# Row lists of a routed feed-forward layer: one-hot products with the operands exchanged

## The reference, cut to what matters

```python
logits = xf @ Wr + br                      # (4096, 8)
Sm = softmax(logits, axis=-1)
G_t, idx_t = top_k(Sm.T, n_tok // E)       # 512 tokens of each expert
tokens = xf[idx]                           # gather
mid = silu(einsum('keh,ehf->kef', tokens, Wu) + bu)
out = einsum('kef,efh->keh', mid, W_down) + b_down
y = zeros_like(xf).at[idx].add(G[..., None] * out)
```

## Time and profile before

| | us |
|---|---|
| median of 3 runs (lowest, highest) | 440.31 (439.63, 442.09) |
| profiled execution | 442.52 |
| its span, first to last instruction | 440.6 |

### The profile page before, as it was taken

The page is one execution under the profiler, slowest core; times in us unless marked ns, Lnnn a source line. Parts: engine busy times, 40 slices in busy tenths (PEclk is TensorE's granted clock), DMA queues, the critical chain, the costliest instruction groups (busy, mean ns, idle before and its releaser), DMA issues.

```text
span 440.6 us, 5594 instructions
## 1 busy us (share of the span) xinstructions
PE 364.5 (83%) x1631; PEld 241.7 (55%) x1631; DVE 235.1 (53%) x882; ACT 147.7 (34%) x350; POOL 165.2 (37%) x250
## 2 busy tenths in 40 slices
PE   5899999899998980112599999999999999999920
PEld 3788886567775650002337566474655657464610
DVE  2555553787889888887753736513130311059450
ACT  1433332344685884330031120402213030347600
POOL 0310053001467884000343442436334253564853
PEclk9999998999999995555589999989999999999985
DMA  8845443600133554800111352514433162689641
GB/s 276 285 137 177 156 126 117 218 2 1 48 121 105 185 178 137 9 0 2 49 49 51 79 114 61 82 51 99 118 81 50 45 131 87 112 280 372 222 145 48
DMA packets 49631, 50.75 MB, mean 115 GB/s; under 512 B 12138, under 2 KB 42563, under 8 KB 49603
## 3 DMA queue, kind: packets, MB, share of 16 engines
q1 hardware_dynamic: 43650, 40.32, 30.2%
q0 software_dynamic: 5952, 10.10, 11.4%
HBM read 32.97 MB, written 17.43 MB: 114 GB/s over the span
## 4 chain that ended last, share of the span: by engine, by line
PE 62%; DVE 14%; POOL 10%; issue 6%; DMA 3%; ACT 1%; POOLq 0%; SPq 0%; DVEq 0%; ACTq 0%
PE ps L808 16%; PE ps L779 15%; PE ps L614 6%; PE ps L622 6%; PE ps L598 6%; PE ps L753 4%; PE ps L692 3%; POOL rstd L1390 3%; DVE qexp L1016 2%; PE ps L705 2%; DMA out<-h_all 1%; PE ps L766 1%; DMA heads<-ysum,idx 1%; POOL ysum L1443 1%; DVE ht_all L1132 1%
## 5 line engine op out<-in xcount | busy, mean ns | idle before, releaser
L808 PE MATMUL ps<-wdn_s,ht_all 128*128 128x256 f32 (+1 forms) x384 | 97.0, 399 | 0.0
L779 PE MATMUL ps<-xgt,wup_s 128*128 128x512 f32 (+1 forms) x192 | 88.7, 615 | 0.0
L808 PEld LDWEIGHTS ps<-wdn_s,ht_all 128*128 128x128 f32 (+1 forms) x384 | 68.9, 192 | 25.5 <-issue 18.4
L1338 ACT ACTIVATE ht_all<-ps,bup_s 128x512 f32<-128x512 f32 (+1 forms) x48 | 33.0, 687 | 126.8 <-PE ps L779 126.8
L1436 POOL DMA_INDIRECT xg<-table,idx x32 | 32.4, 1013 | 92.1 <-DVE idx L1139 54.1
L779 PEld LDWEIGHTS ps<-xgt,wup_s 128*128 128x128 f32 (+1 forms) x192 | 33.7, 184 | 47.9 <-issue 47.9
L1443 POOL DMA_INDIRECT ysum<-yb,idx x24 | 40.6, 1690 | 48.2 <-DVE yb L1170 42.7
L1170 DVE TENSOR_SCALAR yb<-ps,gate 128x256 f32<-128x256 f32 x24 | 11.6, 484 | 57.4 <-PE ps L808 57.4
L598 PE MATMUL ps<-wqkv_s,heads 128*128 128x264 f32 x128 | 33.1, 406 | 7.0 <-DMA heads<-xt 5.2
L705 PE MATMUL ps<-wp_s,turned 128*128 128x264 f32 x128 | 33.7, 385 | 0.0
L598 PEld LDWEIGHTS ps<-wqkv_s,heads 128*128 128x128 f32 x128 | 25.5, 201 | 11.9 <-issue 7.3
(11 more groups left out here) (189 smaller groups left out, 519.1 us busy)
## 6 DMA issues: line engine op xcount, KB each, us to landing
wdn_s<-wdn SPq DMA_DIRECT2D x8, 640.0 KB
heads<-xt SPq DMA_DIRECT2D x8, 512.0 KB, 3.7
h_all<-x SPq DMA_DIRECT2D x8, 512.0 KB, 5.9
ht_all<-xtq SPq DMA_DIRECT2D x8, 512.0 KB, 3.7
table<-x SPq DMA_DIRECT2D x32, 128.0 KB, 1.7
ysum<-x SPq DMA_DIRECT2D x32, 128.0 KB, 1.8
h_all<-ysum SPq DMA_DIRECT2D x8, 512.0 KB, 8.7
out<-h_all SPq DMA_DIRECT2D x8, 512.0 KB, 6.1
```

What stands on the lines that cost most here:

```text
L779: mm = pe.matmul(ps[0:width, f % 2, :], wup_s[:, c, f * P:f * P + width], xgt[:, c, :], start=(c == 0), stop=(c == C - 1))
L808: mm = pe.matmul(ps[:, bank, 0:D], mid[0:rows_, f, j * P:(j + 1) * P], wdn_s[0:rows_, f, :], start=(f == 0), stop=(f == FT - 1))
L1338: act.activation(mid[0:width, f, :], ps[0:width, f % 2, :], ACT.Silu, bias=bup_s[0:width, e // GS, f:f + 1]).then_inc(s_mid, 1)
```

## The change

A slot is split into 64 partition parts and 8 column parts. `hot` has 64 one-hot values for each tile (128 x 2048), `pay` 16 columns. In the 32 products the operands are exchanged: 16 columns of `pay` are the weights, and 64 columns of `hot`, 64 bytes apart, are streamed, into 16 partitions x 64 columns of PSUM. ScalarE copies this (`keep_shares`) into a memory that is free by then; two f32 products with the 16 x 64 shares as weights and 8 constant columns (C_ROWS) turn it into 64 partitions each, once into the lower and once into the upper half. `numbers` reads 8 columns as before. In an expert the order on TensorE is `shared_lists(e + 2)`, `turn(e + 1)`, `whole_lists(e + 2)`; in expert 2 the second part stands behind the second row block of the down product, and `numbers(4)` behind the second product with the gates.

```diff
+KD = 2 * KT
+SLOTS = KSEL // KD
...
+    for half in range(2):
+        for value in range(2):
+            for j in range(KT):
+                c[value * KD + half * KT + j, C_ROWS + half * KD + value * KT + j] = 1.0
...
-        hot = dead[:, FT * KSEL:FT * KSEL + NT * P // 2].bitcast(BF16).rearrange("p (k s) -> p k s", s=NT)
-        iotas = sb("iotas", [P, P, NT], BF16)
+        hot = dead[:, FT * KSEL:FT * KSEL + NT * SLOTS // 2].bitcast(BF16).rearrange("p (k s) -> p k s", s=NT)
+        iotas = sb("iotas", [P, SLOTS, NT], BF16)
...
-        eq4 = sb("eq4", [P, NT, KT])
-        pay = sb("pay", [P, NT, 2, KT], BF16)
+        eq4 = sb("eq4", [P, NT, KD])
+        pay = sb("pay", [P, NT, 2, KD], BF16)
...
+        shares = junk[0:2 * KD, 4, 0:SLOTS]
...
-            def lists(e):
+            def shared_lists(e):
                 pe.wait_ge(s_hot, e + 1)
                 for s in range(NT):
-                    mm = pe.matmul(ps[:, 6, 0:2 * KT], hot[:, :, s], pay[:, s].rearrange("p w k -> p (w k)"),
+                    mm = pe.matmul(ps[0:2 * KD, 6, 0:SLOTS], pay[:, s].rearrange("p w k -> p (w k)"), hot[:, :, s],
                                    start=(s == 0), stop=(s == NT - 1))
+                mm.then_inc(s_sharemm, 1)
+
+            def whole_lists(e):
+                pe.wait_ge(s_share, e + 1)
+                for half in range(2):
+                    at = C_ROWS + half * KD
+                    mm = pe.matmul(ps[half * SLOTS:(half + 1) * SLOTS, 6, P:P + KD], shares, cs[0:2 * KD, at:at + KD],
+                                   start=True, stop=True)
                 mm.then_inc(s_idmm, 1)
...
                 if e + 2 < E and e != 2:
-                    lists(e + 2)
+                    shared_lists(e + 2)
                 if not last:
                     turn(e + 1)
+                if e + 2 < E and e != 2:
+                    whole_lists(e + 2)
...
                     if e == 2 and j == 0:
-                        lists(4)
-
-            lists(0)
+                        shared_lists(4)
+                    if e == 2 and j == 1:
+                        whole_lists(4)
+
+            shared_lists(0)
+            whole_lists(0)
             for r in range(2):
                 count_second(r)
             turn(0)
-            lists(1)
+            shared_lists(1)
+            whole_lists(1)
...
-                dve.tensor_scalar(part_i[:], slot_i[:], KT.bit_length() - 1, None, ALU.arith_shift_right).then_inc(s_slot, 1)
-                dve.tensor_scalar(four_i[:], slot_i[:], KT - 1, None, ALU.bitwise_and).then_inc(s_slot, 1)
+                dve.tensor_scalar(part_i[:], slot_i[:], KD.bit_length() - 1, None, ALU.arith_shift_right).then_inc(s_slot, 1)
+                dve.tensor_scalar(four_i[:], slot_i[:], KD - 1, None, ALU.bitwise_and).then_inc(s_slot, 1)
...
-                dve.tensor_tensor(hot, part.to_broadcast([P, P, NT]), iotas[:], ALU.is_equal).then_inc(s_hot, 1)
+                dve.tensor_tensor(hot, part.to_broadcast([P, SLOTS, NT]), iotas[:], ALU.is_equal).then_inc(s_hot, 1)
...
-                dve.tensor_copy(idp[:], ps[:, 6, 0:2 * KT]).then_inc(s_idp, 1)
+                dve.tensor_copy(idp[:], ps[:, 6, P:P + KD]).then_inc(s_idp, 1)
...
-                    if e == 2 and j == 0:
+                    if e == 2 and j == 1:
                         numbers(e + 2)
...
+            def keep_shares(e):
+                act.wait_ge(s_sharemm, e + 1)
+                act.copy(shares, ps[0:2 * KD, 6, 0:SLOTS]).then_inc(s_share, 1)
+
             def expert(e):
                 for f in range(FT):
                     up(e, f)
+                if e + 2 < E and e != 2:
+                    keep_shares(e + 2)
                 turn(e + 1)
+                if e == 2:
+                    keep_shares(e + 2)
 
             act.sem_inc(s_mid, 2)
+            keep_shares(0)
             turn(0)
+            keep_shares(1)
...
-            pool.tensor_copy(iotas[:], cs[:, C_IOTA:C_IOTA + P].unsqueeze(2).to_broadcast([P, P, NT])).then_inc(s_iotas, 1)
+            pool.tensor_copy(iotas[:], cs[:, C_IOTA:C_IOTA + SLOTS].unsqueeze(2).to_broadcast([P, SLOTS, NT])).then_inc(s_iotas, 1)
```

More of the change, by code:

```diff
@@ L79 @@
 C_FOUR = C_HEAD8 + HH
-C_TILE = C_FOUR + KT
+C_TILE = C_FOUR + KD
 C_PART = C_TILE + NT
@@ L85 @@
 C_PICK = C_NEG + 2 * TB
-C_ALL = C_PICK + P
+C_ROWS = C_PICK + P
+C_ALL = C_ROWS + 2 * KD
 R_BK, R_BP, R_GAMMA, R_BETA = (D * i for i in range(4))
@@ L109, in constants @@
     c[:, C_HEAD8:C_HEAD8 + HH] = p[:, None] // HD == np.arange(HH)
-    c[:, C_FOUR:C_FOUR + KT] = np.arange(KT)
+    c[:, C_FOUR:C_FOUR + KD] = np.arange(KD)
     c[:, C_TILE:C_TILE + NT] = np.arange(NT)
@@ L359, in build @@
         s_idmm = sem("s_idmm")
+        s_sharemm = sem("s_sharemm")
+        s_share = sem("s_share")
         s_idp = sem("s_idp")
@@ L1121, in spread @@
             def spread(e):
-                shape = [P, NT, KT]
+                shape = [P, NT, KD]
                 part = part_f[:, e:e + 1, :]
                 dve.tensor_tensor(eq4[:], four_f[:, e, :].unsqueeze(2).to_broadcast(shape),
-                                  cs[:, C_FOUR:C_FOUR + KT].unsqueeze(1).to_broadcast(shape), ALU.is_equal).then_inc(s_eq4, 1)
+                                  cs[:, C_FOUR:C_FOUR + KD].unsqueeze(1).to_broadcast(shape), ALU.is_equal).then_inc(s_eq4, 1)
                 dve.wait_ge(s_eq4, e + 1)
```

## The result

The kernel with the change took 462.63 us (median of 4 runs, 461.44 to 464.62), the kernel before beside it 440.87 (4 runs, 439.63 to 442.09): a ratio of 1.0494, with a 95% interval of 1.0453 to 1.0536. That is 21.8 us slower, where 12.1 were forecast. The profiled execution took 462.39 us, its span is 460.6. Where the clock fell is known from this execution alone; its mean granted clock is 0.899, that of the other three runs 0.896 to 0.903.

A forecast was written before the change was run, and what follows sets the result against it. TensorE was taken to bound the expert loop, each list paid in full. Loop +11.0, before it +1.7, clock -0.6 gave +12.1 us: 452.4 us on the median (454.6 for the profiled execution), range 436.8 to 458.0.

The forecast's parts named there:

- the two causes that it named: Expert loop: slower list steps, +0.99 us, and edges with small products, +0.85 us a list; six lists +11.0 us.
- What bounds the kernel: Expert loop: TensorE is the path, lists are paid in full; loading 128 one-hot weights sets a step's 62 ns.
- The 32 steps: Each list on TensorE: a step goes from 62 to 93 ns, +0.99 us a list, between -0.99 and +1.5.
- the upper bound of 109: List step on TensorE: slowest step allowed for, 109 ns, +1.5 us a list.
- The two rivals, 54 and 31 ns: List step: stream half as slow, 54 ns, 443.5 us, chance 0.27; free of stride costs, 31 ns, 439.1 us, 0.28.
- the free stride: List stream without stride costs: 31 ns a step in the loop, 439.1 us with a tail to 435, chance 0.28.
- The edges: TensorE around each list: weight-shape changes 0.64 us plus four small f32 passes 0.22, together +0.85, between 0.12 and 1.2.
- The clock: Passes after list 1: clock rises at the same instant, a later start gives back 0.6 us, between 0 and 2.9.
- VectorE, ScalarE, the covers: One-hot rows fall to 1.19 us, worth nothing for lists 2 to 7; turning passes cover ScalarE's copy in the loop.
- Before the loop: Lists 0 and 1, ahead of the expert loop: the first up product starts +1.7 us late.
- The three small operations: VectorE, each list: 128 to 256 elements, +0.14 us each, a little under 0.4 together.

The follow-up runs named there:

- The packed stream: The changed kernel with the 64 streamed one-hot columns of a step side by side (before 64 bytes apart): 437.56 us, ratio 0.9915 to the kernel before.
- the run with the list in halves: The changed kernel with 16 of a list's 32 steps ahead of the turning passes and 16 behind (list 4 whole): 461.56 us, one run.
- the sweep of the stream: The changed kernel with the streamed one-hot columns spaced differently by list, 2 to 64 bytes (64 in lists 0, 1, 4): 448.9 us, one run.
- that of the weights: The kernel before with the 128 one-hot weights spaced differently by list, 2 to 64 bytes (64 in lists 0, 1, 4): 439.06 us, one run.

## Why the prediction was wrong

The direction held, and so did the place and the order of the two causes that it named. The size didn't: +22.2 in the stretch where +12.1 were forecast, because of a third cause that it put at nothing in the loop, the clock. By its steps:

**What bounds the kernel: its reading failed in part.** A list is paid in full in the loop, as said. But "not the array's columns set it, but the loading of 128 one-hot weights" is only half of it: a step with 128 weights takes 25 ns where they lie 4 bytes apart or less. It was the spacing, and the change carried it over to the operand that pays nearly four times as much a line.

**The 32 steps: mechanism right, term too small.** Strided reads were taken as dear, at 93 ns from a VectorE cast strided by 16 bytes; the runs show 110, just past the upper bound of 109, at both clocks. Six lists: +9.8 instead of +6.0. That a VectorE price came this near is luck: no run ties it to TensorE's, which is 116 ns a step at those 16 bytes. The two rivals, 54 and 31 ns, are refuted by the 110. The packed stream's 29 ns is what the free stride would have given.

**The edges: too large.** 0.85 a list was forecast, 0.49 measured. The loader's idle time is there, as forecast, ahead of the turning and the small products (weight loads after in order of time, idle before in brackets):

```profile
236.80 0.85 PEld L785 LDWEIGHTS ps<-cs,xg 128*128 128x128 f32 x8 [0.22 <-issue]
237.83 0.19 PEld L772 LDWEIGHTS ps<-cs,qexp 16*64 16x64 f32 x4 [0.17 <-issue]
```

But the turning lost only 0.09 us (1.02 for 0.93), the first down block 0.19, and the four small passes took 0.21 with their edge: the two halves stand in different columns of the array and run side by side (their passes start 7 ns apart, at 237.828 and 237.835, 237.907 and 237.914 us), so there is no edge between them. The lists' miss of +3.8 and the edges' of -2.3 cancel in part, which is luck too.

**The clock: the step that failed.** The prediction gave it -0.6 us, and looked for it only before the loop; there it came out (-0.5). It needed the clock to rise at the same instant as before, and it did, between 224 and 225 us; but in the run with the list in halves, which is the same up to there, it rose between 227 and 228, and these 16 passes took 9.67 us and not 9.26. In the loop, where the prediction put the clock at nothing, it cost +7.4, by far the largest miss: without it the kernel would have taken about 455 us, inside the range of 436.8 to 458.0. The kernel before already had it: 0.50 behind list 4, with TensorE busy without a gap. It was within reach in the view of stretches, and the prediction looked at the clock of list 1 and list 6 only the earlier trace rows.

**VectorE, ScalarE, the covers: right.** The one-hot op takes 1216 ns (1.19 us forecast; its fixed part, taken as 100 ns from no row, comes out at 2 x 1216 - 2283 = 149), ScalarE's copy 202 ns, and in the waits from 200 to 400 us (total us, times, longest) TensorE waits for both only at lists 0 and 1:

```profile
PE ps L763 <- DVE ht_all L1157: 3.9, 2, 3.7
...
PE ps L772 <- ACT qexp L1369: 0.6, 2, 0.3
```

**Before the loop: too small** by 1.0 us in the table, whose stretch starts at the one-hot rows and leaves out list 0's three small operations, which the forecast's +1.7 includes. These grew from 0.81 to 1.15 us (in the chain the first starts at 202.41 before and 200.60 after, the one-hot rows at 203.22 and 201.75). So the miss is 1.4, which is what two lists of 3.69 in place of 2.98 come to. The three small operations were taken as "a little under 0.4"; 3 x 0.14 is 0.42, and 0.34 was measured.

Together the misses in the table are 7.4 + 3.8 - 2.3 + 1.0 = 9.9 of the 10.1 us between 12.1 and 22.2.

**What stays open.** Slow steps took the clock away behind 6 of 6 lists where they lasted 3.9 to 4.1 us of about 62 ns a step, behind 4 of 6 in the changed kernel, 2 of 6 with list halves, 1 of 4 slow ones in the sweep of the stream (lists 4 to 7), 1 of 3 in that of the weights (lists 4, 6 and 7), and 1 of 6 before: each time in the one profile that there is of a kernel. List 4, which alone stands between two row blocks of the down product, is the one hit where only one is; with list halves it was not hit. Why some slow lists are hit and others not, the runs don't tell; a slow stretch is a risk, and the 7.4 us is what the three falls that the kernel before didn't have (behind lists 5, 6 and 7) cost in this profile.

## What to carry to other kernels

Before the operands of a small product are exchanged, look at how many 16-byte lines a step reads on each side: the price went by them, and laying the tile index out so that neighbouring elements lie 4 bytes apart gained more (2.1 to 2.4%) than the exchange in any form. Interleave two and not one, where the engine that writes the tile needs it. When slow steps of TensorE get longer, look at the granted clock of the stretch behind them in the kernel before: what it shows once may come after every such stretch.

## What the runs showed of the hardware

A streamed bf16 element 16 to 64 bytes from the next costs TensorE 1.7 to 1.8 ns (at 64 bytes, 110 ns a step, at 2.4 and at 1.2 GHz alike); a weight so spaced 0.45 to 0.48. A pair of 128 packed weights and 8 columns passes in 25 ns at the clock of 1.00; the Trainium skill, TensorE: Matmul & The Clock Gate, "Back-to-back issue gap", has about 25 ns as the floor for up to 64 columns. These runs bear it out for packed operands, at 25 ns with 8 columns and 29 with 64; the strided stream's 110 lies far above it. The granted clock fell to 0.50 where the profile has TensorE without idle time, behind lists of about 60 and of 110 ns a step, and in the loop never behind those of 25 to 33 ns. VectorE's comparison in bf16 against an operand that repeats along the innermost index ran at half speed (2285 ns for 2048 elements, 4418 for 4096); with two tiles interleaved it ran at full speed (1219 and 2284).
